# Reordering the prologue of a one-core decoder kernel: the gated values' chain first, one weight split on GpSimd, first taps and one weight part later

## The reference

```python
# 1: gated mixer with a state of 16
h   = silu(conv4(x @ in_w.T + in_b) + conv_b)           # 512 channels, 4 causal taps
xp  = h @ xp_w.T + xp_b                                  # 32 columns
a   = exp(-exp(xp[..., :16]));  b = silu(xp[..., 16:]) * sum(h)
ys  = scan(state * a + b);      x1 = layernorm(x + ys @ out_w.T + out_b)
# 2: cross attention; ctx (77 rows a batch) and x1 are the keys, 8 heads of 128
kv  = concat([LN(ctx), LN(x1)]) @ Wkv + bkv;  q = LN(x1) @ Wq + bq
x2  = layernorm(x1 + softmax(q k^T / sqrt(128)) v @ Wo + bo)
# 3: mixture of 8 experts, top 2, capacity 512 tokens per expert
y   = layernorm(x2 + combine(relu(tokens @ W1.T) @ W2.T))
```

## Time and profile before

| | |
|---|---|
| median of 3 runs | 1027.61 us (1026.38 to 1028.1) |
| the profiled execution's own time | 1027.42 us |
| its span | 1025.7 us |
| TensorE busy | 979.9 us, 96% of the span |
| VectorE busy | 809.4 us, 79% |
| ScalarE busy | 729.3 us, 71% |
| GpSimd busy | 568.7 us, 55% |

### The profile page before, as it was taken

The page is one execution under the profiler, slowest core; times in us unless marked ns, Lnnn a source line. Parts: engine busy times, 40 slices in busy tenths (PEclk is TensorE's granted clock), DMA queues, the critical chain, the costliest instruction groups (busy, mean ns, idle before and its releaser), DMA issues.

```text
span 1025.7 us, 21471 instructions
## 1 busy us (share of the span) xinstructions
PE 979.9 (96%) x7018; PEld 929.5 (91%) x7018; DVE 809.4 (79%) x2040; ACT 729.3 (71%) x1865; POOL 568.7 (55%) x967
## 2 busy tenths in 40 slices
PE   8999999999999999999999999999999999999960
PEld 7799999999999999999999999999999999899960
DVE  6887878887888888888888888878887877655526
ACT  6686868787777777776877787868786766365536
POOL 4743464656566556554656566545656463526543
PEclk9999999999999999999999999999999999999985
DMA  7643031213111311113110311041105110386448
GB/s 248 220 135 110 6 118 36 61 35 108 47 50 46 101 53 51 45 59 96 51 45 30 125 51 46 17 137 50 47 11 171 33 41 11 140 293 126 67 60 315
DMA packets 63829, 89.60 MB, mean 87 GB/s; under 512 B 14932, under 2 KB 44680, under 8 KB 63720
## 3 DMA queue, kind: packets, MB, share of 16 engines
q1 hardware_dynamic: 56040, 75.51, 22.8%
q0 software_dynamic: 7680, 12.72, 5.8%
HBM read 49.21 MB, written 38.99 MB: 86 GB/s over the span
## 4 chain that ended last, share of the span: by engine, by line
PE 77%; ACT 8%; DVE 6%; issue 3%; DMA 3%; POOL 1%; SPq 0%; ACTq 0%; DVEq 0%; POOLq 0%
PE ps L611 20%; PE ps L612 20%; PE ps L613 20%; PE ps L640 7%; PE ps L719 3%; DVE nmx L1800 2%; DMA accd<-yo,tku 1%; ACT fx L1378 1%; PE ps L655 1%; PE ps L757 1%; PE ps L657 1%; POOL accd L2174 1%; ACT hp L1076 1%; ACT ys_x L1179 1%; ACT prob L1237 1%
## 5 line engine op out<-in xcount | busy, mean ns | idle before, releaser
L2085 POOL TENSOR_SCALAR prob<-prob,rinv 128x333 f32<-128x333 f32 x256 | 144.4, 575 | 242.1 <-DVE rinv L1809 241.1
L1232 ACT ACTIVATE oT_hi<-ps 128x256 fp32r<-128x256 f32 x126 | 48.5, 385 | 151.4 <-PE ps L657 151.4
L611 PE MATMUL ps<-kv_lo,w_hi 128*128 128x256 f32 (+1 forms) x512 | 154.4, 302 | 1.1 <-DVE kv_lo L1386 1.1
L613 PE MATMUL ps<-kv_hi,w_hi 128*128 128x256 f32 (+1 forms) x512 | 153.4, 300 | 0.0
L612 PE MATMUL ps<-kv_hi,w_lo 128*128 128x256 f32 (+1 forms) x512 | 153.1, 299 | 0.0
L1237 ACT ACTIVATE prob<-ps,nmx 128x333 f32<-128x333 f32 x256 | 135.0, 538 | 7.4 <-DVE nmx L1800 7.4
L1386 DVE TENSOR_TENSOR pT_lo<-ps,pT_hi 128x512 fp32r<-128x512 f32 x254 | 131.8, 550 | 1.1 <-ACT pT_hi L1249 0.3
L1800 DVE TENSOR_REDUCE nmx<-ps 128x2 f32<-128x666 f32 x128 | 108.3, 846 | 9.3 <-PE ps L613 7.9
L640 PE MATMUL ps<-ident,prob 128*128 128x128 f32 (+1 forms) x768 | 105.5, 272 | 1.8 <-POOL prob L2085 1.0
L611 PEld LDWEIGHTS ps<-kv_lo,w_hi 128*128 128x128 f32 x512 | 96.9, 189 | 1.6 <-issue 1.5
L612 PEld LDWEIGHTS ps<-kv_hi,w_lo 128*128 128x128 f32 x512 | 96.5, 189 | 0.0
(11 more groups left out here) (308 smaller groups left out, 3284.6 us busy)
## 6 DMA issues: line engine op xcount, KB each, us to landing
wraw<-in_W SPq DMA_DIRECT2D x14, 512.0 KB, 7.9
vcd_hi<-vst_hi SPq DMA_DIRECT2D x10, 512.0 KB, 2.7
vcd_lo<-vst_lo SPq DMA_DIRECT2D x10, 512.0 KB, 3.5
v_hi<-vcd_hi SPq DMA_DIRECT2D x32, 154.0 KB
v_lo<-vcd_hi SPq DMA_DIRECT2D x32, 154.0 KB
slots<-initr SPq DMA_DIRECT2D x8, 520.0 KB, 7.8
xs<-in_x SPq DMA_DIRECT2D x16, 256.0 KB, 4.4
xts<-in_xT SPq DMA_DIRECT2D x15, 256.0 KB, 4.1
```

The lines of the kernel that those rows point to most:

```text
L611: pe.matmul(dst, hi1, lo2, start=first, stop=False, skip_group_check=True)
L613: return pe.matmul(dst, hi1, hi2, start=False, stop=last, skip_group_check=True)
L2085: pool.tensor_scalar(prob[:, h % 2, t, 0:KEYS], prob[:, h % 2, t, 0:KEYS], rinv[:, h % 2, t:t + 1], 1.0, ALU.mult, ALU.mult).then_inc(norm ...
```

## The change

In VectorE's `first()`: `context_stats(1)` moves from before `silu(0, 1)` to behind the scan; the two instructions that make `oww_x` leave; `split_lo([2])` moves from behind the scan to behind `latents`, where `split_lo([4])` was; `split_lo([4])` moves behind `latents_hi`, next to `split_lo([5])`. GpSimd's `first()` takes the two `oww_x` instructions, between `context_lo(0)` and `context_norm(1)`. In ScalarE's, `tanh_half(-1, 1)` is ahead of `split_hi([1])`, `unit("in", 0, 1)` is ahead of `split_hi([2])`, `split_hi([3])` is behind `state_hi`, and `first_tap(1, 0)` and `first_tap(1, 1)` move from in front of `unit("ln")` to places behind it. In TensorE's, the transposes of context tile 1 (`unit("cT", 0, 1)`, with its wait) move from in front of the value biases to behind them, and `idle_turns(14, ...)` becomes `idle_turns(10, ...)`.

```diff
@@ tensor: first()
                 unit("vc", 0, 0, 0, ps[:, 0, :])
                 unit("vc", 1, 0, 0, ps[:, 4, :])
-                pe.wait_ge(cxf_set, 1)
-                unit("cT", 0, 1, 0, ps[:, 6, :])
                 pe.wait_ge(bvb_set, 1)
                 value_bias(range(0, 3))
                 pe.wait_ge(owx_set, 5)
...
                 pe.matmul(ps[:, AVB, 0:D], ap(ones[0:1, :]), bor[:], start=False, stop=True).then_inc(cvec_mm, 1)
+                pe.wait_ge(cxf_set, 1)
+                unit("cT", 0, 1, 0, ps[:, 6, :])
                 pe.wait_ge(hp_set, 4)
-                idle_turns(14, S0 + 1)
+                idle_turns(10, S0 + 1)
                 pe.wait_ge(cxf_set, 2)
                 unit("ln", 0, 0, 0, ps[:, 6, :])
@@ scalar: first()
                 split_hi([0])
                 tanh_half(-1, 0)
+                tanh_half(-1, 1)
                 split_hi([1])
-                tanh_half(-1, 1)
-                split_hi([2, 3])
                 unit("in", 0, 1, 0, ps[:, 0, :])
+                split_hi([2])
                 act.wait_ge(small_ld, 48)
                 unit("xp", 0, 0, 0, ps[:, 2, :])
                 unit("in", 1, 1, 0, ps[:, 1, :])
                 state_hi(-1)
+                split_hi([3])
                 unit("vc", 0, 0, 0, ps[:, 0, :])
                 unit("vc", 1, 0, 0, ps[:, 4, :])
                 unit("cT", 0, 1, 0, ps[:, 6, :])
                 split_hi([4, 5])
-                first_tap(1, 0)
-                first_tap(1, 1)
                 unit("ln", 0, 0, 0, ps[:, 6, :])
                 split_hi([6])
                 unit("vc", 0, 1, 0, ps[:, 2, :])
+                first_tap(1, 0)
                 unit("k", 0, 0, 0, ps[:, 7, :])
                 split_hi([7])
                 unit("q", 0, 0, 0, ps[:, 5, :])
                 unit("vc", 1, 1, 0, ps[:, 4, :])
+                first_tap(1, 1)
                 unit("v", 0, 0, 0, ps[:, 7, :])
@@ vector: first()
                 context_hi(0)
-                context_stats(1)
                 silu(0, 1)
                 split_lo([0, 1])
-                dve.wait_ge(oww_ld, 48)
-                dve.wait_ge(owx_set, 3)
-                dve.tensor_copy(oww_x[:], oww[:]).then_inc(owx_set, 1)
-                dve.wait_ge(owx_set, 4)
-                minus(oww_x[64:96, :], oww[64:96, :], oww_x[64:96, :]).then_inc(owx_set, 1)
                 unit("xp", 0, 0, 0, ps[:, 2, :])
                 scan(-1, 1, 0)
-                split_lo([2])
+                context_stats(1)
                 state_lo(-1, 1)
...
                 latents(-1, 1, 0)
-                split_lo([4])
+                split_lo([2])
                 dve.wait_ge(cvec_mm, 1)
                 dve.tensor_copy(cvec[:], ps[:, AVB, 0:D]).then_inc(cvec_set, 1)
                 latents_hi(-1, 1, 0)
-                split_lo([5])
+                split_lo([4, 5])
@@ gpsimd: first()
                 context_lo(0)
+                pool.wait_ge(oww_ld, 48)
+                pool.wait_ge(owx_set, 3)
+                pool.tensor_copy(oww_x[:], oww[:]).then_inc(owx_set, 1)
+                pool.wait_ge(owx_set, 4)
+                pool.tensor_tensor(oww_x[64:96, :], oww[64:96, :], ap(oww_x[64:96, :]),
+                                   ALU.subtract).then_inc(owx_set, 1)
+                pool.wait_ge(owx_set, 5)
                 context_norm(1)
```

## The result

The changed kernel takes 1030.03 us (median of 20 runs, 1027.76 to 1032.33), the kernel before 1027.77 us beside it (20 runs, 1026.38 to 1029.41). The ratio is 1.0020 with a 95% interval of 1.0013 to 1.0027: 2.3 us slower, with an interval of 1.3 to 2.8. The prediction was +1.0, to 1028.6, with a whole range of 1026.2 to 1030.3: the sign was right, the size a little under half of what came. The result lies above the forecast's own range (1027.8 to 1029.5) and above the 1029.7 from which the prediction would call it slower, an outcome that it gave 14%. It is inside the whole range only because that one reached up for a rival that did not come true. One execution of the kernel before, beside experiments 1 to 4, took 2515 us and is in no comparison.

The account below looks back on a forecast made before the run. A data chain bounds the prologue, then TensorE sets the pace. -0.1 for `lnp` and +1.2 for the second low part give +1.1 at q: 1028.6 us predicted, own range 1027.8 to 1029.5, whole range 1026.2 to 1030.3.

Parts of the forecast that it names:

- The two chains level at q: In the prologue, q waits both for k and for VectorE's fifth low part, which ended 0.13 before q began.
- 4.25 us of unbroken TensorE work: From q to the first scores TensorE runs without gaps, so a later q shifts the scores equally, to 38.3.
- The early part: Ahead of the residual sum: xp 17.17 to 16.25, context units at 18.5, `op` at 22.5 against 23.64.
- costed at nothing: The `oww_x` pair on GpSimd behind cx_lo ends by 22.0 at the latest, before `op` at 22.5, so adds nothing.
- the mutual exclusion: Two-input VectorE instructions and GpSimd's SBUF reads exclude each other; x1 on GpSimd ends 1.1 later, hidden.
- The whole gain is spent on the way to `lnp`: Between residual sum and `lnp`, GpSimd's queue and tile 1's later transposes use up 1.1 us; `lnp` at most 0.1 earlier.
- The late GpSimd queue: Rival: cxn on GpSimd takes 2.79 rather than 1.24, making `lnp` 1.55 later; +2.65, 1030.2 us; 12%.
- batch 0's gaps take the shift: Rival: TensorE's 0.81 us of gaps in the first body absorb part of the delay; +0.3, 1027.9 us; 13%.
- the carried gain: Rival: q does not wait for the low parts, so the early gain is carried whole; -1.1, 1026.4 us; 12%.
- The taps on ScalarE: Batch 1's first taps fill ScalarE's waits ahead of k_hi and v_hi, costing nothing; about 1.1 us if cover fails.

Follow-up runs that it names:

- experiment 2: The kernel before with only chunk 2's low part moved behind latents and chunk 4's behind latents_hi: 1028.57 us, ratio 1.0009 to the kernel before.
- experiment 1: The changed kernel with chunk 2's low part right behind state_lo and chunks 4 and 5 placed as before the change: 1027.21 us against 1027.42, ratio 0.9998.
- experiment 4: The changed kernel with eight unread transposes on TensorE ahead of q's wait: 1028.19 us, ratio 1.0008 to the kernel before.
- Experiment 3: The changed kernel with the two oww_x instructions back on VectorE, behind the low parts of chunks 0 and 1: 1029.99 us, ratio 1.0018 to the kernel before.
- experiment 7: The changed kernel with GpSimd's powers ahead of chunk 3's low part: 1030.97 us, ratio 1.0020 to the kernel before.
- experiment 8: The changed kernel with both first taps back ahead of unit("ln") on ScalarE: 1031.73 us against 1027.81 for the kernel before, ratio 1.0034.
- experiment 6: The kernel before with chunk 2's and 4's low parts moved and 8 idle turns between k and q: 1029.58 us against 1028.87, ratio 1.0012.
- experiment 5: The changed kernel with tile 1's statistics, its transposes, the low parts and the oww_x pair re-placed, meant to be faster: 1029.71 us against the kernel before's 1028.87.

## Why the prediction was right in kind and short in size

**The two chains level at q: right.** VectorE's queue, with one low part more behind `kv_lo`, set q. The term was +1.2 for that part, +1.1 at q; measured +1.11 behind k, in the changed kernel and alone in experiment 2. Putting the part back removes it (experiment 1).

**"4.25 us of unbroken TensorE work" behind q: the step that failed.** It took the row of before for a constant, but that row was read at a granted clock of 1.00. In the profile of the changed kernel the clock fell in the very idle time that I forecast, to the 1.2 GHz level for 3.4 us, and the stretch took 5.74. The term that was missing is +1.4 to +1.5 (experiment 4: 1.38 with the same start of q; experiment 2: 1.39). None of my rivals had it. The Trainium skill (TensorE: Matmul & The Clock Gate, the table "Why this matters for your kernels") would not have supplied it: it names a length that the idle gaps between bursts should stay under, and each gap here is well under that. By it the clock would have stayed at 1.00 and the scores would have come at 34.28 + 4.25 = 38.53; they came at 40.02. Measurement and that row of the page differ, and the measurement decides: the clock fell in the last of three gaps of 1.28, 1.11 and 0.97 us, and in experiment 2 in the last of two of 1.11 and 0.96.

**The early part: right in direction, with two terms mis-sized.** xp started at 15.90, not 16.25 (its chain of taps also ended earlier in this execution: the second silu half stood at 15.16 and not at 15.53). The `oww_x` pair, "costed at nothing", was bounded by its own length on GpSimd, and that bound held: it ended at 17.85 + 1.59 = 19.44 and nothing waited for it. What I left out is what it and `cx_lo` do to VectorE beside them: the low parts took 3.09 instead of 2.35, so the context units began at 18.90 and `op` at 22.91, each 0.4 later than forecast although VectorE had begun 0.37 earlier. Experiment 3, with the pair away, leaves 2.88: so some 0.2 of these 0.74 go with the pair, and the other 0.53 with `cx_lo`, in that run the only instruction of GpSimd beside them. I had used the mutual exclusion only in one direction, for GpSimd's `cxn` and `x`. There it held: `x`, which meets two low parts, took 4.70 us from 31.61, against 3.65 before, and this is not on the way to the scores.

**"The whole gain is spent on the way to `lnp`": right.** `lnp` came at 27.74, against 27.4 forecast and 27.52 before. The forecast had `a_rs` ending at 27.35; it ended at 27.47, with a further wait that no term named: `a_vv` on VectorE was held for 0.9 us until chunk 3's low part on GpSimd had ended. The other path was late too: `cfull` ended at 27.50, not at 27.0, since `op` and the transposes behind it were 0.4 later than forecast. By experiment 7 that block can't be ordered away by swapping two entries: with the powers first, `cx_hi` is held instead for 1.35. Here the Trainium skill (SBUF — State Buffer, "Who interferes with whom") says that casts and tensor-scalar operations of VectorE, too, can take the port pair that it shares with GpSimd, and that the one that issues first keeps it for its whole instruction. The traces agree: 0.16 against 1.04, and 0.28 against 1.63.

**The rivals.** The late GpSimd queue (+2.65) gave nearly the right time by the wrong path, so that the result is still inside the whole range is luck: `cxn` lasted 1.21 and met nothing, and `lnp` was 0.2 late, not 1.5. That batch 0's gaps take the shift is refuted by the body's windows, and the carried gain by q's wait. The taps on ScalarE cost nothing that the trace shows, as forecast, and experiment 8 shows what they would have cost where they stood.

**What is accounted for.** In the profile: 0.2 ahead of k, 1.1 idle, 1.5 clock, together 2.8 of 3.5; the other 0.7 lie ahead of the second expert's adds, behind a DMA, and their cause stays open. In the medians: 2.3 with both parts, 0.8 with the clock kept (experiment 4), -0.2 with the order put back (experiment 1); each of the last two has an interval of about 0.9 either way. That the order of the low parts makes the loss is clear in the medians (experiment 1 against the changed kernel); the clock's own share is seen in the profiles, and the medians are too wide to part it from the gap's. No version measured here is measurably faster than the kernel before.

## What to carry to other kernels

A new wait of TensorE has two prices: its length, and what the work behind it costs if the granted clock falls. Price the stretch behind the wait at both levels, and look whether a few idle transposes in front of a wait that can't be avoided keep the clock: in the profiles of experiments 4 and 6 it stayed at 1.00, though a gain in the medians isn't shown. Where VectorE and GpSimd work side by side from SBUF, moving work from one to the other can still cost the one that gave it away: look at which instruction stands beside it, the small ones on the critical chain above all. And before advancing a chain, look at what its consumer waits for next; here that was VectorE's low parts, in the same place as before.

## What the runs showed of the hardware that was not expected

The granted clock fell to 0.50 in the second of two idle times of TensorE, of 1.11 and 0.96 us with 1.2 us of matmuls between them (experiment 2), and came back 3.4 us later. It stayed at 1.00 in the profile of experiment 1, behind idle times of 1.76 and 1.11 us with 2.0 us of matmuls between them, and at q in experiment 7. What decides it was not settled, nor in how many executions of one kernel it happens.

A VectorE instruction on a tile of 128x2 lasted 1.04 us (experiment 1: 1.57) instead of 0.16 while a long instruction of GpSimd was under way, and ended with it: at 26.31 against 26.28, in experiment 1 at 27.36 against 27.33. The delay was the rest of the other engine's instruction, not a matter of the small one's size.

The start of batch 0's chain differs between profiled executions by more than most edits here are worth: xp at 15.90 in the changed kernel, 16.44 in experiment 1 and 17.99 in experiment 5, with the same work ahead of it up to the order of small pieces. Differences between two lines of one trace repeat better than absolute times of the prologue: from k to q it was 2.12, 2.12 and 2.11 us in the changed kernel and experiments 2 and 3.
